# Layer 2 of a graph layer in split float32: the order of the high and the low products on TensorE

## What is computed

```python
h = jnp.maximum(_layernorm(x, axis=-1), 0.0)
agg = segment_sum(edge_features, tgt, 50000) / max(counts, 1)   # (50000, 64)
combined = jnp.concatenate([agg, h], axis=1)                    # (50000, 320)
h1 = jax.nn.relu(combined @ W1 + b1)                            # W1 (320, 512)
out = x + (h1 @ W2 + b2)                                        # W2 (512, 256)
```

## Time and profile before

| | us |
|---|---|
| median of 3 runs | 1337.73 (1337.44 to 1338.54) |
| the profiled execution's own time | 1335.77 |
| its span | 1334.2 |
| PE busy in the span | 1320.6 (99%) |
| PE weight loads busy | 1117.5 (84%) |
| DVE busy | 1214.9 (91%) |
| ACT busy | 697.1 (52%) |
| POOL busy | 541.3 (41%) |

### The profile page before, as it was taken

The page is one execution under the profiler, slowest core; times in us unless marked ns, Lnnn a source line. Parts: engine busy times, 40 slices in busy tenths (PEclk is TensorE's granted clock), DMA queues, the critical chain, the costliest instruction groups (busy, mean ns, idle before and its releaser), DMA issues.

```text
span 1334.2 us, 29281 instructions
## 1 busy us (share of the span) xinstructions
PE 1320.6 (99%) x6994; PEld 1117.5 (84%) x6994; DVE 1214.9 (91%) x3153; ACT 697.1 (52%) x1285; POOL 541.3 (41%) x707
## 2 busy tenths in 40 slices
PE   7999999999999999999999999999999999999998
PEld 4788888888888888888888888888888888888887
DVE  6899999999999999999999999999999999999997
ACT  5445454545454545454545454545454555555553
POOL 6443434343434343434343434343434343434341
PEclk9999999999999999999999999999999999999999
DMA  4676767676767676767676767676767676767663
GB/s 119 126 138 118 137 120 136 120 136 120 136 120 135 121 135 122 134 122 133 123 132 124 131 125 130 126 129 127 128 128 127 129 126 130 125 131 124 132 111 76
DMA packets 420693, 168.21 MB, mean 126 GB/s; under 512 B 319092, under 2 KB 420230, under 8 KB 420680
## 3 DMA queue, kind: packets, MB, share of 16 engines
q1 hardware_dynamic: 419688, 166.89, 67.4%
q10 hardware_dynamic: 992, 1.18, 0.4%
HBM read 66.25 MB, written 51.40 MB: 88 GB/s over the span
## 4 chain that ended last, share of the span: by engine, by line
PE 94%; SPq 2%; DMA 1%; issue 1%; DVE 1%; POOL 0%; ACT 0%; DVEq 0%; POOLq 0%
PE P L945 26%; PE P L947 13%; PE P L922 13%; PE P L924 13%; PE P L923 13%; PE P L931 6%; PE P L932 6%; PE PA L911 1%; PE PA L910 1%; SPq L328 1%; DMA HQ<-HN 1%; SPq L329 1%; SPq L316 1%; PE P L968 0%; PE PA L906 0%
## 5 line engine op out<-in xcount | busy, mean ns | idle before, releaser
L945 PE MATMUL P<-w_both,H_hi 128*128 128x512 f32 x1564 | 548.3, 392 | 2.3 <-DVE H_lo L737 2.1
L615 ACT ACTIVATE H_hi<-P 128x512 fp32r<-128x512 f32 x392 | 233.8, 597 | 490.0 <-PE P L932 490.0
L947 PE MATMUL P<-w_both,H_lo 128*128 128x256 f32 x1564 | 437.8, 280 | 0.0
L945 PEld LDWEIGHTS P<-w_both,H_hi 128*128 128x128 f32 x1564 | 292.5, 187 | 69.1 <-DVE H_lo L737 3.4
L737 DVE SCALAR_TENSOR_TENSOR H_lo<-P,H_hi 128x512 fp32r<-128x512 f32 x392 | 265.9, 679 | 67.4 <-ACT H_hi L615 64.4
L922 PE MATMUL P<-HT_hi,w_hi 128*128 128x512 f32 x776 | 309.0, 398 | 0.0
L923 PE MATMUL P<-HT_lo,w_hi 128*128 128x512 f32 x776 | 303.3, 391 | 0.0
L924 PE MATMUL P<-HT_hi,w_lo 128*128 128x512 f32 x776 | 303.2, 391 | 0.0
L464 POOL TENSOR_TENSOR XB<-X,b_row 128x1024 f32<-128x1024 f32 x97 | 234.0, 2413 | 166.9 <-DVE O L751 166.0
L947 PEld LDWEIGHTS P<-w_both,H_lo 128*128 128x128 f32 x1564 | 295.2, 189 | 3.6
L458 POOL TENSOR_TENSOR E_both<-ES,E_both 128x256 fp32r<-128x256 f32 x98 | 72.7, 742 | 392.0 <-ACT E_both L595 392.0
(11 more groups left out here) (87 smaller groups left out, 1194.1 us busy)
## 6 DMA issues: line engine op xcount, KB each, us to landing
out_dram<-O SPq DMA_DIRECT2D x97, 512.0 KB, 4.6
HQ<-HN SPq DMA_DIRECT2D x384, 128.0 KB, 3.9
X<-in_x_dram SPq DMA_DIRECT2D x95, 512.0 KB, 4.3
ER<-in_edge_attr_dram SPq DMA_DIRECT2D x392, 32.0 KB, 1.8
DT<-table_dram SPq DMA_DIRECT2D x392, 1.0 KB, 1.7
X<-in_x_dram ACTq DMA_DIRECT2D x1, 512.0 KB, 5.2
w_raw<-in_L_gnn_W_dram ACTq DMA_DIRECT2D x4, 128.0 KB, 5.5
w_raw<-in_L_gnn_W_dram SPq DMA_DIRECT2D x2, 256.0 KB, 4.8
```

What stands on the lines that cost most here:

```text
L615: act.activation(H1_hi[:, m, nodes(t)], bank(m)[:, nodes(t)], ACT.Relu).then_inc(s_1hi, 1)
L945: pe.matmul(out_bank(j)[some, :], H1_hi[:, m, rows], w2_both[:, m, :, :].rearrange("p a d -> p (a d)"), start=(m == 0), stop=False)
L947: last = pe.matmul(out_bank(j)[some, 0:D], H1_lo[:, m, rows], w2_both[:, m, 0, :], start=False, stop=(m == CH - 1))
```

## The change

In `layer2` the loop over the chunks of a group is split in two: first all products with `H1_hi` (512 moving columns), then all with `H1_lo` (256). With `j == 0` each product with `H1_hi` waits for `s_1hi` and each with `H1_lo` for `s_1lo`; before, the pair waited for `s_1lo` ahead of the first. In tile 0 a wait for `s_hlo` to reach 4 is added ahead of layer 2.

```diff
                     for m in ms:
                         if j == 0:
-                            pe.wait_ge(s_1lo, CH * t + m + 1)
-
+                            pe.wait_ge(s_1hi, CH * t + m + 1)
                         pe.matmul(out_bank(j)[some, :], H1_hi[:, m, rows], w2_both[:, m, :, :].rearrange("p a d -> p (a d)"),
                                   start=(m == 0), stop=False)
+                    for m in ms:
+                        if j == 0:
+                            pe.wait_ge(s_1lo, CH * t + m + 1)
                         last = pe.matmul(out_bank(j)[some, 0:D], H1_lo[:, m, rows], w2_both[:, m, 0, :],
                                          start=False, stop=(m == CH - 1))
...
                 if isinstance(t, int) and t == 0:
                     pe.wait_ge(s_whi, 4)
                     pe.wait_ge(s_wlo, 2)
+                    pe.wait_ge(s_hlo, 4)
                 layer2(t)
```

## The result

| | before | changed |
|---|---|---|
| median, 12 runs each | 1336.38 us | 1338.70 us |
| span of the profiled execution | 1334.2 us | 1337.3 us |
| start to start of a tile in the loop | 13.360 us | 13.393 us |

The ratio is 1.0028, 95% interval 1.0015 to 1.0040, so the change makes the kernel slower by about 2.3 us (medians) to 3.1 us (spans). I had forecast no difference; slower by over 0.2% had a chance of 0.09. Without the two, the means are 1338.4 and 1336.5 us, still 1.8 us slower.

The account below looks back on a forecast made before the run. PE was taken as the bound, busy 1320.6 of 1334.2 us, product after product from 61.12 us on. Order, waits and added waits summed 0 + 0 + 0, so 1337.7 us was forecast, range 1334.6 to 1340.2.

Parts of the forecast that it names:

- Part 1, "I take 110, and so no cost": Layer 2's new order: weight loads follow at 110 ns, within the low product's 117.7 ns slot; cost zero.
- my upper end: Low behind low in layer 2: loads need 120 ns, 2.3 ns over the slot, 977 times, 2.2 us slower.
- the prediction's own sign: Loop tiles: the forecast is wrong if the tile's period moves by over 28 ns; pairs should stay at 347 ns.
- Is 117.7 ns the product's own time.: Layer 2 low products: whether alternation inflates their 117.7 ns; taken as zero, lower end 0.8 us gained.
- Rival B: Layer 2: alternating makes the low product 117.7 ns instead of 114.6, so 1332.9 us; chance 0.06.
- Part 2, the waits: Stalls near 61 and 1304 us: 0.23 us gained at each, lost again at L931 waiting for QA; net zero.
- Rival A: Ahead of L945: all idle time comes back, 2.3 us, giving 1335.4 us; chance 0.04.
- Part 3, the added waits: Layer 2: eight waited products a full tile instead of four; waits already met cost nothing.
- rival D: Waited low products in layer 2: loads lie bare, 392 x 0.11 = 43 us slower, 1380.8 us; chance 0.05.
- Rival E: Runs of lows in layer 2: loads need their full 189 ns row, 70 us slower, 1407 us; chance 0.04.
- rival C: Layer 2: faster, with low products at 115 ns or less as its sign; chance 0.01.
- The high end of the range, 1340.2: Whole kernel: 1337.7 + 2.2 = 1339.9 us, with 0.3 us for the spread of the runs 1340.2.

Follow-up runs that it names:

- f3: Against the kernel before: grouped order (highs, then lows), with low products of 128 columns instead of 256; one execution, 1332.10 us.
- e2_waits_only: Kernel before with only the change's waits, order still high, low alternating; 1335.47 us, ratio 0.9993.
- e4_groups01: Kernel before with only chunks 0 to 2 of node groups 0 and 1 reordered, waits of before; 1341.89 us, ratio 1.0043.
- f4_merged: Kernel before with the highs of two node groups ahead of the lows of both (runs of 6, 2 and 8); 1345.79 us, ratio 1.0080.
- g1_edges_after_chunk0: Kernel before with the seven small edge-means products after chunk 0 of layer 1 instead of chunk 1; 1379.63 us, ratio 1.0325.

## Why the prediction was wrong

**Part 1, "I take 110, and so no cost".** This step failed, twice over. First, the lows. In the changed kernel the ten products behind another low are 118.9 ns from their successors on average, against 116.7 for a low in the alternating order. That is 2.2 ns, close to the 2.3 ns of my upper end; its source, twice the 60 ns of the 64-column loads, was nearer the measurement, in part by luck, since the lows in runs stand anywhere from 113 to 120 ns and the first of a run is faster than the rest. The transposes at 110 ns have streams of 128 columns (and `f3` has 111 to 114 for loads behind such short ones). I took that interval as one that would also hold under a stream of 256 columns, and no row showed it. All 16 lows of a tile take 1882.7 ns instead of 1866.6, 16.1 more.

Second, the highs, for which the sum had no term. I followed only the slot of the low product and took 229.2 ns for every high one as given. In layer 2 the highs were 3684.2 ns a tile and became 3703.1: 18.9 ns, over half of the loss. The high products right behind a run of lows, at 233 and 236 ns in groups 1 and 3 and at 236 in chunk 3 of group 0, are 24 ns over the 230.0 of before; others are a little faster. The row was there: after the last pair of layer 2 the products of layer 1 begin with two such distances, 612.75 being followed, in means, by 233.4 and 235.8 before they fall to 228.9. The 13 that I averaged begin three products later. 16.1 + 18.9 - 1.6 in layer 1 is the 33 ns.

Behind both stands one premise, that a kind of product has one distance, which a row of before can give. The runs show that it has several, by what stands ahead: the first L945 of a tile has 229.2 ns, the second 235.0, the others 230.0. By the prediction's own sign, a period that moves by over 28 ns, it is wrong; pairs in layer 2 take 349.1 ns on average where it wanted 347.

**"Is 117.7 ns the product's own time."** The split was off by 1 ns: in the alternating order it is 230.0 + 116.7, not 229.2 + 117.7. Rival B, which had alternating dearer than runs, is wrong at this width (layer 2 takes 346.9 ns a pair alternating, 349.1 grouped). At 320 columns the grouped layer 2 is the faster one, by 2.3 ns a pair, two thirds of it in the highs.

**Part 2, the waits: right.** Both stalls gave a shorter wait at layer 2 and a longer one at L931 (0.51 us at the first, where I had 0.49, and 0.52 at the second, where 0.28 + 0.23 makes 0.51), and `e2_waits_only` moved the time by nothing that can be told (ratio 0.9993). Rival A is out.

**Part 3, the added waits: right.** No distance moved by them by more than 0.1 ns (`e2_waits_only`), which also ends rival D with its 110 ns a wait.

**Rival E: the right place, the wrong size.** It named low behind low as the place and 120.5 ns as the point from which it decides. It stays under that point, at 118.9; at the price of 70 us it is out, since the loads of `f3` follow at 111 to 114 ns and last 188 to 192. No run shows the term behind rival C's 0.01, 256-column lows in a run that go well under the 117.7 ns of the alternating order: in no run of such lows was a single distance below 111 ns, and the lowest mean that a run held was 115.8, in every second tile of `e4_groups01`.

The high end of the range, 1340.2, did hold the time as such, 1338.70. That is luck in part, since the kernel before came out at 1336.38 and not at the 1337.73 from which the range was built. The ratio to the kernel before is what counts, and there I forecast no difference where there is one: the ends of two estimates of a few ns, times a thousand products, should have made "slower" a leading case and not 0.09.

## What to carry to other kernels

Where PE is busy all the time, as here at 99%, an order of products is a matter of nanoseconds times thousands (349.1 ns a pair against 346.9, in 1564 pairs): measure the distance between starts for each kind of neighbour, ahead and behind, before calling a reordering free, and give the products behind the reordered ones a term as well. Judge a new order by the whole kernel, since the price may be paid in a stretch that was not edited, and may change its sign with the width (33 ns a tile lost at 256 columns, 80 saved at 320). Look at single tiles as well as at means: the same stretch had two times in one execution here (13.363 and 13.517 us a tile in `e4_groups01`), and a mean of both belongs to neither. And follow a loosened wait up to the next operand that the same engine waits for; if the slack ends there, it was worth nothing, like the 0.2 us that L931 waited longer here.

## What the runs showed that I had not expected

Streams of equal products with equal loads settled into repeating rhythms in these runs, and there were several. With 512 columns: 226.7 ns each (the last six of the run of eight in `f4_merged`), a cycle of three of 229.2, 231.7 and 225.9 (layer 1 in nearly all kernels, its lines L922, L923, L924, L931 and L932 all taking part, so it isn't the operands), and 233.4 (the first half of layer 1 in `f4_merged`). With alternating 512 and 256 columns: 346.7 or 353.6 ns a pair. The granted clock was 1.00 in the stretches of all these profiles. Which rhythm came went with what stands ahead: tile after tile it is the same to about 1 ns in most kernels, takes turns in `e4_groups01`, and in `g1_edges_after_chunk0` it changed in three tiles, with how layer 1 had ended.

Why there are several, and what sets them, stays open: no run here changes only the moment at which a load starts. No order of the full work tried here beat the kernel before by more than a measurement can tell.
